# Storing the one-hot rows of the head blocks in DRAM, and moving the last addition of the messages to VectorE, in a four-layer graph network

## What is computed

```python
for _ in range(2):                                   # hops
    head_emb, tail_emb = e[head], e[tail]
    rel_emb = relation_emb[relation_type]
    ricci = l2_normalize(tail_emb + rel_emb)
    hyper_head = expmap0(head_emb)
    hyper_tail = expmap(tail_emb, hyper_head)
    hyper_rel = expmap(rel_emb, hyper_head)
    res = project(mobius_add(hyper_tail, hyper_rel))
    res = relu(logmap(res, hyper_head) + ricci * 1e-7)
    e = l2_normalize(segment_mean(res, head))
    out = 0.5 * out + e
```

## Time and profile before

| | us |
|---|---|
| median of 3 runs | 24344.68 |
| lowest and highest | 24342.23, 24354.15 |
| the profiled execution's own time | 24370.34 |
| its span | 24368.5 |
| POOL busy | 16775.5 (69%) |
| PE busy | 12002.2 (49%) |
| DVE busy | 9424.1 (39%) |
| ACT busy | 2083.8 (9%) |

### The profile page before, as it was taken

The page is one execution under the profiler, slowest core; times in us unless marked ns, Lnnn a source line. Parts: engine busy times, 40 slices in busy tenths (PEclk is TensorE's granted clock), DMA queues, the critical chain, the costliest instruction groups (busy, mean ns, idle before and its releaser), DMA issues. The chain is left out here.

```text
span 24368.5 us, 206631 instructions
## 1 busy us (share of the span) xinstructions
PE 12002.2 (49%) x52285; PEld 10009.4 (41%) x52286; DVE 9424.1 (39%) x14053; ACT 2083.8 (9%) x3841; POOL 16775.5 (69%) x16828
## 2 busy tenths in 40 slices
PE   3233434677757777576764435344334434334333
PEld 1111222566646666466663335333333323333333
DVE  6555444688868888511111112111111121111112
ACT  0000001233322322100010001000000000000000
POOL 4777777788847777577727772777477757774775
PEclk6555566555555555555555555555555555555555
DMA  0000001222222222211111111111211121121112
GB/s 23 2 2 10 26 25 50 51 59 57 57 42 56 56 55 56 38 27 27 27 14 28 28 28 13 28 28 28 21 28 28 28 27 28 28 26 23 28 28 27
DMA packets 756517, 765.78 MB, mean 31 GB/s; under 512 B 442786, under 2 KB 522854, under 8 KB 736348
## 3 DMA queue, kind: packets, MB, share of 16 engines
q0 software_dynamic: 528384, 511.86, 13.4%
q1 hardware_dynamic: 227932, 251.96, 3.3%
HBM read 659.46 MB, written 103.37 MB: 31 GB/s over the span
## 5 line engine op out<-in xcount | busy, mean ns | idle before, releaser
L447 POOL DMA_INDIRECT rows<-table_lin,pay x9984 | 9444.2, 946 | 4814.9 <-issue 3026.1
L1427 DVE TENSOR_TENSOR acc<-acc,pair 128x1024 f32 x832 | 1016.1, 1221 | 10646.5 <-PE pair L671 10604.7
L671 PE MATMUL pair<-rows,onehot 128*128 128x64 f32 x19968 | 4798.9, 425 | 0.0
L671 PEld LDWEIGHTS pair<-rows,onehot 128*128 128x128 f32 x19968 | 4492.3, 332 | 520.3 <-issue 520.3
L659 PE MATMUL pair<-ones_bf,zeros_bf 1*128 1x512 bf16 x1664 | 837.6, 604 | 7794.9 <-issue 7789.6
L447 POOL DMA_INDIRECT rows<-table_hyp,pay x3328 | 3324.8, 999 | 1240.9 <-issue 993.8
L659 PEld LDWEIGHTS pair<-ones_bf,zeros_bf 1*128 1x128 bf16 x1664 | 109.8, 100 | 7923.2 <-issue 7923.2
L431 POOL DMA_INDIRECT payload_src<-rows x1600 | 1559.2, 974 | 738.8 <-issue 738.8
L634 PE MATMUL pair<-tab,sel_t 128*128 x6656 | 1560.0, 409 | 979.1 <-ACT head L832 404.9
L431 POOL DMA_INDIRECT payload_dst<-rows x1600 | 1563.5, 977 | 499.0 <-issue 487.5
L634 PEld LDWEIGHTS pair<-tab,sel_t 128*128 128x128 f32 x6656 | 1366.0, 304 | 1263.3 <-issue 1263.3
(11 more groups left out here) (301 smaller groups left out, 15183.3 us busy)
## 6 DMA issues: line engine op xcount, KB each, us to landing
rows<-table_lin,pay POOLq DMA_INDIRECT x9984, 2.4
rel<-rel_rows SPq DMA_DIRECT2D x52, 1072.0 KB
xs<-rel_rows SPq DMA_DIRECT2D x52, 1072.0 KB
rows<-table_hyp,pay POOLq DMA_INDIRECT x3328
rel_rows<-rel SPq DMA_DIRECT2D x26, 1072.0 KB
rel_rows<-xs SPq DMA_DIRECT2D x26, 1072.0 KB
payload_src<-rows POOLq DMA_INDIRECT x1600, 2.1
payload_dst<-rows POOLq DMA_INDIRECT x1600
```

Of the source, the lines that this page charges most:

```text
L447: pool.indirect_dma_start(out=rows[:, h, t, 0:width], out_offset=None, in_=table[:, :], in_offset=bass.IndirectOffsetOnAxis(ap=pay[:, h, t ...
L671: last = nc.tensor.matmul(sums[:, bass.ds(at, D)], onehot[:, h, t, :], mv, start=False, stop=False, skip_group_check=True)
L1427: V.tensor_tensor(flat_acc[:, at], flat_acc[:, at], ps_half[u], ALU.add)
```

## The change

The one-hots of the head's place are made once, in the sorting stage, and stored in DRAM (`head_hots`, 104 halves of 1 MB). DVE makes them next to the relations' one-hots, half by half in two buffers that both `h` share (`hot_half`, in the room of `msg` and `onehot`), each after the store of what was there. SP stores them ahead of the two stores of `rel_rows` of the pair. In passes 0 and 1 SP loads a group's 2 MB in one DMA (`load_hot`) after its relations' load and after both halves' sums of the older group in the same buffer (`scattered`); PE's turning waits for that load in place of DVE's `hot_made`. `make_half_hot` makes only the relations' one-hots.

POOL's `mix` is left with the multiplication, now in halves, each with its `mixed`. DVE waits for it and does the addition itself. The ReLU waits for DVE's `coefficients` in place of `mixed`, and so does SP's load of the relations. The semaphores `transposed` and `sel_copied` are shared by both passes.

```diff
+        head_hots = nc.dram_tensor("head_hots", (2 * GROUPS, P, HG * P), FP32, kind="Internal").ap()
...
+        hot_half = [flat_msg[:, 0:HG * P], flat_hot[:, 5900:5900 + HG * P]]
...
+            def store_hot(i, h, u):
+                await_reg(sp, "sp", types_made, 6 * i + (3 * h + u + 2))
+                sp.dma_start(head_hots[bass.ds(4 * i + (2 * h + u), 1)].rearrange("a q c -> (a q) c"), hot_half[u]).then_inc(hot_moved[h][u], 16)
+
+            def load_hot(m, i, h, free):
+                if free:
+                    await_reg(sp, "sp", scattered, 4 * i + (m * SUMMED + 2 * h - 2))
+                sp.dma_start(onehot[:, h, :, :].rearrange("p (u t) n -> p u (t n)", u=2),
+                             head_hots[bass.ds(4 * i + 2 * h, 2)].rearrange("a q c -> q a c")).then_inc(hot_moved[h][0], 16)
...
                 for h in range(2):
+                    for u in range(2):
+                        store_hot(i, h, u)
+                for h in range(2):
                     store_rel(i, h)
...
-                            await_reg(sp, "sp", S["mixed", m], MIXES * 2 * i + MIXES * (h - 1))
+                            await_reg(sp, "sp", S["coefficients", m], MIXES * 2 * i + MIXES * (h - 1))
                             load_rel(i, h)
+                            load_hot(m, i, h, True)
...
             def mix(m, g, h):
-                hd, rl = head[h][:, :, 0:D], rel[h][:, :, 0:D]
-                await_reg(pool, "pool", S["coefficients", m], MIXES * g + 1)
-                nc.gpsimd.tensor_tensor(rl, rl, over(EO[:, 3, :], D), ALU.mult).then_inc(S["mixed", m], 1)
-                await_reg(pool, "pool", S["mixed", m], MIXES * g + 1)
                 for u in range(2):
-                    await_reg(pool, "pool", S["coefficients", m], MIXES * g + (u + 2))
-                    nc.gpsimd.tensor_tensor(hd[:, half(u), :], hd[:, half(u), :], rl[:, half(u), :], ALU.add).then_inc(S["mixed", m], 1)
+                    rl = rel[h][:, half(u), 0:D]
+                    if u == 0:
+                        await_reg(pool, "pool", S["coefficients", m], MIXES * g + 1)
+                    nc.gpsimd.tensor_tensor(rl, rl, over(EO[:, 3, half(u)], D), ALU.mult).then_inc(S["mixed", m], 1)
...
-                if q % (QG // 2) == 0:
-                    await_reg(pe, "pe", hot_made, 2 * g + (m * HOT + q // (QG // 2) + 1))
+                if q == 0:
+                    await_reg(pe, "pe", hot_moved[h][0], 16 * i + ((m + 1) * LOADED + 16))
...
-                        await_reg(act, "act", S["mixed", m], MIXES * g + (u + 2))
+                        await_reg(act, "act", S["coefficients", m], MIXES * g + (u + 2))
                         nc.scalar.activation(res, res, ACT.Relu).then_inc(S["answered", m], 1)
...
+                for u in range(2):
+                    for k in range(2):
+                        if k < h or turned:
+                            await_reg(dve, "dve", hot_moved[k][u], 16 * i + (16 if k < h else 0))
+                    V.tensor_tensor(hot_half[u].rearrange("p (t n) -> p t n", n=P), over(pay[:, h, half(u), 1], P),
+                                    ps_sort_iota.unsqueeze(1).to_broadcast([P, HG, P]), ALU.is_equal)
+                    dve.drain().then_inc(types_made, 1)
...
                     level()
-                    TT(th, th, tr, ADD)
+                    ttl(th, th, tr, ADD)
+                    await_reg(dve, "dve", S["mixed", m], 2 * g + (u + 1))
+                    TT(th, th, rl[:, half(u), 0:D], ADD)
                     dve.drain().then_inc(S["coefficients", m], 1)
                 dve.sem_inc(rows_free, 1)
...
                 t = half(u)
-                V.tensor_tensor(onehot[:, h, t, :], over(pay[:, h, t, 1], P),
-                                ps_iota.unsqueeze(1).to_broadcast([P, HG, P]), ALU.is_equal)
                 V.tensor_tensor(type_hot[:, h, t, :], over(pay[:, h, t, 2], R),
```

## The result

The changed kernel takes 24753.5 us (median of 4 runs, 24748.15 to 24762.49), the kernel before 24345.0 us in the same series: a ratio of 1.0168, with 1.015 to 1.0185 as its interval. It is slower by 408 us; the forecast was slower by 360. The profiled execution's span is 24760.7 us, 392.2 us more than before. The page's engine shares say only that POOL works 510 us less, DVE 222 and PE 148, and ACT 8 more.

What follows compares the result with a forecast made beforehand. POOL and DVE were taken to run at one beat, now closed into a ring of 0.36 + 2.66 + 41.5 + 10.07 = 54.6 us; 360 us more over both passes gave 24705 us, range 24530 to 24900.

Steps and rivals of the forecast that it cites:

- The ring of POOL and DVE: Passes 0 and 1: rows free, payload, gathers, multiplication, DVE's tail, rows free again; 54.6 us a group.
- Case D: Rival: POOL starts the next gathers without DVE's tail; POOL's 45.4 us is the beat, 23775 us; chance 0.06.
- DVE's first new addition: In DVE's tail: held up by POOL's second multiplication, ends 4.77 us behind the gathers, 2.7 us instead of 1.2.
- Case B: Rival: DVE's new addition gets in before POOL's second multiplication; beat 53.0 us, 24540 us; chance 0.12.
- The gathers: POOL's train of 32 per group, stretched beside DVE's two-SBUF-operand multiplications: 41.5 us, against 39.7 bare.
- The one-hots' load: One 2 MB DMA per group: 7.2 us from issue to semaphore, covered by 4.7 us, not binding up to 12 us.
- Case C: Rival: the 2 MB load and the copies behind it bind, from over 12 us; at 15 us 25015; chance 0.13.
- A: Main case: closed chain of waits through POOL and DVE, beat 52.5 to 56.1 us, 24595 to 24855 us; chance 0.64.
- ring 1: Later name for POOL's forecast chain: rows free, payload, gathers, multiplication, DVE's tail; forecast at 54.6 us.
- ring 2: PE's chain, named after measuring: ReLU and sums, one-hots' load, fetch with ACT's copies, and back; 55.12 us in one group.
- The sorting stage: Stage before pass 0: DVE's 208 added one-hot makes, 500 us, covered by its idle time; 0 cost, at most 15 us.
- The sum: Pass 0 217 us, pass 1 133 us, first freed row 5 us in each pass: together 360 us more.

## Why the prediction was right, and where its reasons were not

**The ring of POOL and DVE: right.** It is there with the terms forecast (0.35, 2.72, 41.57 and 10.22 us against 0.36, 2.66, 41.5 and 10.07), POOL idles 9.8 us ahead of the first gather in the mean (490.4 / 50; 9.4 forecast), and DVE's additions alone bring 371 us. Case D, an open ring, is out.

**DVE's first new addition: right.** It took 2.80 us (2.7 forecast), behind a wait of 4.1 us in the mean (about 5 forecast), and ended 1.09 us behind POOL's two multiplications, the same 1.09 us as in the earlier trace rows. Case B did not happen: POOL went from one half to the other without a gap, "x2" in 3.77 us.

**The gathers: right, and the row was the better guide.** The row shows gathers of 1.28 and 2.00 us beside DVE's operations with two SBUF operands; the second ends 0.82 us behind `L1308`. By the Trainium skill, "SBUF — State Buffer", section "Who interferes with whom", such operations leave descriptor writing alone, which it marks as inferred. The trace shows gathers held up nevertheless, and the beat of 52.8 us that was worked out from the rule was not seen. A gather also reads its row numbers from `pay` in SBUF, and whether that or the writing is held up no run here tells apart.

**The one-hots' load: the term was mis-sized, and its margin hardly existed.** The forecast followed the load from issue to PE in 7.2 us, to a stall of 3.9 us at the second answer, and to a margin of 4.7 us before it would bind. It took 8.58 us; the stall was 3.8 us in the mean, 6.17 in the group shown. The rows that the 7.2 us were built on give 7.7 (5526.41 to 5531.5, and 2.6 more). The size matters little. The step that failed is the margin: I followed the load only to DVE's coefficients, and not along PE's own queue, where the last fetch step, 3.0 us of issue and the next sums follow, and then the next load. That way closes at 54.4 to 55.1 us, so the margin was under 1 us. Case C had 0.13 and was held to decide from a load over 12 us. In truth C stood beside A: the kernel with only the load lost 358 us. The total came out right because parallel rings do not add up and ring 1 happens to be the longer by under 1 us: as far as the load is concerned, that is luck.

**The rest of the fetch: missed.** In the group shown the first two steps took the 8.8 us of the earlier trace rows (5531.14 to 5539.96), but the forecast did not price the other six, some 3.1 us each; they are 18 of ring 2's 55 us.

**What leaves DVE and POOL bought nothing: right.** DVE's head of messages fell to 0.22 us as forecast, and the gain went into its waits.

**The sorting stage: right in its outcome, wrong in its size.** No scatter was late; the stage ends 7 us earlier. But 52 groups of two halves are 104 makes and 104 stores, not the 208 of the forecast: DVE makes 104 one-hots of 2.29 us, which is the 235 us more that it works, and not 500. So the runs do not show that 500 us would have been covered.

**The sum.** Per pass: 240 and 166 us inside the 49 beats, against 217 and 133 for 50 beats. The beats are 55.15 and 55.34 instead of 54.6. In pass 0 the missing 0.5 us lie nearly all between the payload's load and the first gather, 3.11 us in the mean where 2.66 were forecast, and not in ring 2. The later passes gave back 12.7 us, which the forecast held at zero.

## What to carry to other kernels

Follow a new wait or load along every engine's queue until it comes back to itself: each such ring has its own length, the longest sets the beat, and shortening one when two are equal gains little (56 us of 250 here) until the other is cut too (474 us for both). Where one engine's short step stands behind another's long train, try it inside the train, and tune the place: 26, 28 and 30 of 32 gathers gave 24387, 24147 and 24305 us. One large DMA that waits for both halves of its buffer costs more than two of half the size, of which the first lies under the work on the second half: 24698 against 24280 us with POOL's additions.

## What the runs showed of the hardware

**PE's granted clock was no lower for the waits at the load.** In the group shown above PE stood idle for 8.82 us, and the granted clock was 0.50 (the 1.2 GHz level) over the fetch steps behind it. In the next group it stood idle for 9.59 us, and the clock rose to 1.00 (2.4 GHz) during the steps. Stretches (last columns: granted clock, DMA share, GB/s) and rows of PE in the changed kernel:

```profile
5539.46 2.03 PE L656 MATMUL pair<-tab,sel_t 128*128 x8 [0.22 <-issue]
...
5587.04 1.94 PE L647 MATMUL pair<-ident,onehot 128*128 128x128 f32 x8 [9.59 <-DMA onehot<-head_hots]
...
5592.25 1.13 PE L656 MATMUL pair<-tab,sel_t 128*128 x8 [0.56 <-ACT head L855]
```

```profile
5536.00:5544.00 8.00, 7.29 (x31) 6.37 (x31) 1.75 (x9) 4.28 (x7) 6.17 (x7) 0.50 0.22 48
...
5592.00:5600.00 8.00, 5.54 (x43) 4.85 (x44) 4.53 (x25) 4.84 (x9) 6.13 (x7) 1.00 0.19 40
```

Over the whole stretch from 4500 to 7000 us the granted clock is 0.54 in the kernel before, which never waits for one-hots from DRAM, 0.56 in the changed kernel and 0.55 in the one with half loads. The rows of the first two:

```profile
4500.00:7000.00 2500.00, 1852.18 (x8147) 1610.73 (x8148) 2123.72 (x4743) 764.00 (x1292) 1992.11 (x1727) 0.54 0.25 56
...
4500.00:7000.00 2500.00, 1632.48 (x7434) 1413.36 (x7434) 1747.19 (x4334) 702.34 (x1179) 1621.31 (x1539) 0.56 0.31 90
```

Of the fetch's products in that stretch, 17% run at the higher level in the kernel before, 31% in the changed one and 21% with half loads. A step of eight products takes 2.03 us at the one level and 1.13 us at the other, and the steps follow each other after 3.1 and some 2.3 us.

**A 2 MB load beside gathers** took 8.58 us from SP's issue to PE's first turning. In its fullest microsecond the core moved 451 GB/s, 190 in one of its first:

```profile
5524.00:5525.00 1.00, 0.00 (x0) 0.00 (x0) 0.88 (x3) 0.00 (x0) 0.70 (x2) 0.50 0.81 190
...
5526.00:5527.00 1.00, 0.00 (x0) 0.00 (x0) 0.88 (x2) 0.00 (x0) 0.69 (x2) 0.50 1.06 451
```
